# A new order for the opening of an attention and feed-forward kernel: sign vectors with a semaphore of their own, three matmuls on zeros, one fold block moved, weight splits spread out

## Chip, core and metric

The kernel runs on one core of a Trainium2 chip. The metric is the device time of one execution in microseconds, the median of several runs; less is better.

## What is computed

For each of 8 batch rows of 512 tokens x 256 channels:

```python
xn = layernorm(x)                      # no gain, no bias
x  = x + attention(xn) + ffn(xn)
# attention: 32 query heads, 8 key/value heads, head size 64, rotary embedding,
#   causal with a window of 128 keys, softmax, then @ Wo
# ffn: h = fwht(xn * SU_ug) / 64;  up, gate = h @ W_up.T * s1, h @ W_gate.T * s2
#   y = fwht(silu(gate) * up * SU_dp) / 64 @ W_down.T * s3     (fwht: Walsh-Hadamard transform)
```

All tensors are float32.

## The kernel before

Everything on TensorE that carries data from end to end is done with numbers split in two. A value is kept as `hi` (rounded to the matmul's faster float type) and `lo` (the rest), and each product is three matmuls: hi x hi, hi x lo, lo x hi (lines 948 to 950). ScalarE (ACT) makes the hi part, VectorE (DVE) the lo part. Weights are split once, in the first batch row, and query and output weights are written back to memory in split form and loaded from there for later rows.

The Hadamard transforms are folded into the weights. "Fold k" (`fold_gate_up(k)`, line 1024) multiplies the 512 columns of block k of the gate/up weights by the Hadamard matrix: two output tiles of two matmuls each, and each float32 matmul is two passes, so a fold is eight passes in the trace. ACT (`fold_high`, L587) and DVE (`fold_low`, L787) scale these tiles with the input signs `su_in_sb` and split them; tile n may be computed only when `fold_lo` of tile n - 4 is done. The down weights go through three butterfly levels on GpSimd (POOL, L496 and L498), then through four Hadamard products on TensorE (`down_weights`, L1045), are scaled on DVE (`wd_scale`, L824) and split (`wd_high`, `wd_low`).

Each engine runs its own list in program order, and semaphores tie the lists together. The projections and gate/up products alternate over two PSUM banks; the list `USES` sets whose turn it is, and a bank is written again only when the result before has been read.

The opening of the first row, in order:

- SyncE (SP) issues the loads: x, gate/up block 0, key weights, query weights 0, gate/up block 1, down weights, blocks 2 and 3, and so on. Behind them stand `save_wq(0)`, `save_wq(1)` (each waits for the split of these weights), `stack_k(0)`, `load_wq(b, 2)`, `stack_q(0)`, `load_wq(b, 3)`.
- ACT's own queue issues seven small loads: had, ident, scale_gu, su_in, su_mid, cos, sin. The last five count up one semaphore, `consts_in`.
- DVE computes the statistics of x, waits for all five of `consts_in`, scales the two sign vectors, then normalises x (`row_normalised`, L737), then splits.
- ACT takes the square root for the standard deviation, waits for ident, loads the table for silu (L566), makes the hi parts of the key weights (L594), of the first fold tiles, and of the transposed x (`x_high`).
- TensorE does fold 0, the transposes of x, fold 1, key projection 0 (two parts), query projection 0 (two parts), fold 2, fold 3.
- POOL does butterfly level 0, the rotation of key 0 (it waits for DVE's `products` on the key projection), levels 1 and 2, and then the rotation of query 0.

Then the feed-forward part: for j = 0 to 7 TensorE makes gate j and up j (with the query projections 1 and 2 between them at j = 2 and j = 4) and down j - 2; ACT does `silu(j)` and `h_high(j - 1)`; DVE does `hidden(j)` (L841) and `h_low(j - 1)`. In the first row this is mixed with the down weights behind j = 1, and with splits of query weights 2 and 3 behind j = 3 and j = 7. Query weights 1 and the value weights are split ahead of j = 0. Attention over 8 groups follows, and for later rows the same without the weight work.

## Time and profile before

| | |
|---|---|
| median of 3 runs | 1325.61 us (1322.61 to 1327.97) |
| profiled execution | 1322.25 us, span from first to last instruction 1320.5 us |
| busy, share of the span | PE 1257.2 us (95%), DVE 939.3 (71%), ACT 751.9 (57%), POOL 647.9 (49%) |
| mean granted TensorE clock | 0.995 of full speed |
| first 5 us | no TensorE work; from 5 to 10 us, 2.50 of 5 us |

The profile is one execution, recorded on the chip. A timeline row gives the start and length in us, the engine, the line of the kernel, the operation with output and inputs, a count when equal instructions were merged, and in brackets how long the engine had been idle and what released it. "SPq" and "ACTq" are the issuing sides of the DMA queues of these engines. Rows of PE show matmul passes; weight loads have rows of their own (PEld).

### The profile page before, as it was taken

How to read it: one execution, taken by the hardware profiler on the slowest of the kernel's cores; microseconds unless marked ns; L12 is line 12 of the kernel's file. 1: busy time of each engine (PE TensorE's matmuls, PEld its weight loads, DVE VectorE, ACT ScalarE, POOL GpSimd, SP SyncE). 2: the span in 40 equal slices, each digit the busy share in tenths (PEclk: the TensorE clock that was granted, in tenths of full speed). 3: DMA queues.
4: the chain of work that ended last, by engine and by line, in shares of the span. 5: the costliest groups of instructions: out<-in, count | busy, mean ns of one | idle time of the engine just before them, and what ended most of it. 6: DMA issues, size and time to landing. Idle time of an engine off the chain costs nothing.

```text
span 1320.5 us, 38033 instructions
## 1 busy us (share of the span) xinstructions
PE 1257.2 (95%) x14568; PEld 1063.4 (81%) x14568; DVE 939.3 (71%) x1664; ACT 751.9 (57%) x2814; POOL 647.9 (49%) x655
## 2 busy tenths in 40 slices
PE   7899999999999999999999999999999999999997
PEld 3678888788887888878888788888888888887886
DVE  5668984788648886488854888558874688746875
ACT  3357762577626765267643677346763567625775
POOL 4326652366525654266531665326653366523663
PEclk9999999999999999999999999999999999999999
DMA  6315625144142441424322342323423144141431
GB/s 217 88 52 154 189 83 155 57 126 129 50 144 63 116 130 35 142 80 134 95 89 88 95 134 79 104 73 106 130 90 118 47 117 151 53 142 35 128 97 49
DMA packets 72226, 137.56 MB, mean 104 GB/s; under 512 B 15472, under 2 KB 29296, under 8 KB 72048
## 3 DMA queue, kind: packets, MB, share of 16 engines
q1 hardware_dynamic: 70912, 134.41, 33.6%
q8 instruction: 117, 1.92, 0.6%
q10 hardware_dynamic: 1136, 0.73, 0.2%
q14 instruction: 61, 0.50, 0.1%
HBM read 72.17 MB, written 12.58 MB: 64 GB/s over the span
## 4 chain that ended last, share of the span: by engine, by line
PE 84%; DVE 8%; ACT 6%; issue 2%; DMA 1%; ACTq 0%; DVEq 0%
PE PROJ L948 15%; PE PROJ L950 15%; PE PROJ L949 15%; PE S L1099 10%; PE TR L1113 9%; PE O L1130 5%; PE O L1142 4%; PE TR L1130 4%; ACT e_sb L630 3%; PE S L948 2%; PE S L950 2%; PE S L949 2%; ACT pt_sb L640 1%; DVE S L863 1%; DVE v_mix L906 1%
## 5 line engine op out<-in xcount | busy, mean ns | idle before, releaser
L630 ACT ACTIVATE e_sb<-S,negmax 128x128 f32<-128x128 f32 x1024 | 364.8, 382 | 36.7 <-DVE negmax L865 33.9
L507 POOL TENSOR_TENSOR e_sb<-e_sb,rinv 128x512 f32<-128x512 f32 x256 | 264.8, 1042 | 51.7 <-DVE rinv L870 51.2
L515 POOL TENSOR_SCALAR_AFFINE_SELECT p_cur<-pt_sb 128x512 f32<-128x512 f32 x192 | 122.7, 639 | 275.3 <-ACT pt_sb L640 274.1
L640 ACT ACTIVATE pt_sb<-TR 128x512 f32<-128x512 f32 x256 | 154.8, 605 | 168.0 <-PE TR L1113 168.0
L754 DVE TENSOR_TENSOR prod<-PROJ,rope_sb 128x1024 f32<-128x1024 f32 x160 | 193.2, 1211 | 57.0 <-PE PROJ L950 56.9
L630 ACT ACTIVATION_READ_ACCUMULATOR e_sb<-S,negmax 128x1 f32 x1024 | 225.7, 220 | 0.0
L1113 PE MATMUL TR<-ident,e_sb 128*128 128x128 f32 x1024 | 160.6, 280 | 25.3 <-DVE o_lo L710 15.8
L865 DVE TENSOR_REDUCE negmax<-S 128x4 f32<-128x512 f32 x256 | 177.1, 692 | 8.9
L1099 PE MATMUL S<-k_stack,q_stack 64*64 64x64 f32 (+2 forms) x5632 | 179.8, 266 | 1.7 <-ACT e_sb L630 1.7
L483 POOL TENSOR_TENSOR qy<-prod 128x512 f32<-128x512 f32 x64 | 83.9, 1311 | 177.1 <-DVE prod L754 177.0
L948 PE MATMUL PROJ<-wo_ring,o_hi 128*128 128x256 f32 x512 | 155.0, 303 | 16.0 <-DVE xt_lo L710 14.6
L1113 PEld LDWEIGHTS TR<-ident,e_sb 128*128 128x128 f32 x1024 | 116.9, 141 | 63.6 <-issue 32.8
L1099 PEld LDWEIGHTS S<-k_stack,q_stack 64*64 64x64 f32 x5632 | 160.2, 133 | 8.6 <-ACT e_sb L630 5.7
L624 ACT ACTIVATE staging_rest<-PROJ,scale_gu_sb 128x512 f32<-128x512 f32 x64 | 44.2, 690 | 209.3 <-PE PROJ L950 205.4
L949 PE MATMUL PROJ<-wo_ring,o_hi 128*128 128x256 f32 x512 | 144.6, 282 | 0.0
L950 PE MATMUL PROJ<-wo_ring,o_lo 128*128 128x256 f32 x512 | 144.4, 282 | 0.0
L841 DVE SCALAR_TENSOR_TENSOR p_cur<-PROJ,scale_gu_sb,staging_rest 128x512 f32<-128x512 f32 x64 | 48.1, 751 | 130.4 <-PE PROJ L950 130.4
L858 DVE COPY_PREDICATED S<-diagonal_key,S 128x512 f32<-128x512 int8 x192 | 131.5, 685 | 0.0
L948 PE MATMUL PROJ<-xt_hi,wq_ring 128*128 128x512 f32 x256 | 112.7, 440 | 3.9 <-DVE prod L754 3.0
L948 PEld LDWEIGHTS PROJ<-wo_ring,o_hi 128*128 128x128 f32 x512 | 97.7, 191 | 21.2 <-DVE xt_lo L710 18.0
L781 DVE TENSOR_TENSOR acc<-PROJ,acc 128x512 f32<-128x512 f32 x128 | 87.5, 684 | 31.1 <-PE PROJ L950 31.0
L1130 PE MATMUL O<-pt_sb,v_sb 128*64 128x128 f32 x1024 | 106.0, 285 | 1.4 <-ACT pt_sb L640 1.4
(102 smaller groups left out, 2856.5 us busy)
## 6 DMA issues: line engine op xcount, KB each, us to landing
q_stack<-qy SPq DMA_DIRECT2D x512, 64.0 KB, 2.0
wq_ring<-wq_split_d SPq DMA_DIRECT2D x56, 512.0 KB, 4.7
wo_ring<-wo_split_d SPq DMA_DIRECT2D x56, 512.0 KB, 3.5
k_stack<-ky SPq DMA_DIRECT2D x256, 64.0 KB, 2.7
x_in<-x SPq DMA_DIRECT2D x8, 512.0 KB, 4.4
wq_split_d<-wq_ring SPq DMA_DIRECT2D x8, 512.0 KB, 3.9
wo_split_d<-wo_ring SPq DMA_DIRECT2D x8, 512.0 KB, 3.4
out<-acc SPq DMA_DIRECT2D x8, 512.0 KB, 4.9
```

The source lines that it names most:

```text
L507: nc.gpsimd.tensor_tensor(e, e, r, ALU.mult).then_inc(norm_done, 1)
L630: last = nc.scalar.activation(e_sb[:, n % 2, r, :], s_heads(n, 1)[:, r, :], ACT.Exp, bias=negmax[:, n % 2, r:r + 1], accum_out=rowsum[:, n ...
L640: nc.scalar.activation(pt_sb[:, n % 4, :, :], TR[:, :, :], ACT.Copy).then_inc(t_copied, 1)
L754: nc.vector.tensor_tensor(prod[:, 2 * part:2 * part + 2, :], both, rope_sb[:, :, :], ALU.mult).then_inc(prod_done, 1)
L858: nc.vector.copy_predicated(own.rearrange("p r (a k) -> p r a k", a=2), diagonal_key[:, :, :].rearrange("p r (a k) -> p r a k", a=2), diagonal
L865: nc.vector.tensor_reduce(negmax[:, n % 2, :], own, axis=AX.X, op=ALU.max, negate=True).then_inc(max_done, 1)
L948: nc.tensor.matmul(dst, lhs[0], rhs[0], start=first, stop=False)
L949: nc.tensor.matmul(dst, lhs[0], rhs[1], start=False, stop=False)
L950: return nc.tensor.matmul(dst, lhs[1], rhs[0], start=False, stop=last)
L1099: last = nc.tensor.matmul(dst[:, at:at + (blocks - 1) * step + 1:step, :], q_stack[rows, g % 2, slot, i * P + a * HP:i * P + (a + 1) * HP] ...
L1113: last = nc.tensor.transpose(TR[:, r, :], e_sb[:, n % 2, r, :], ident[:, :])
L1130: last = nc.tensor.matmul(O_half[a][odd * D:(odd + 1) * D, s, :, :], v, pt_sb[:, (2 * pair + s) % 4, odd:REP:2, a * HP:(a + 1) * HP], star ...
```

## The change

The sign vectors are loaded right behind the Hadamard matrix, ahead of the identity, and count up a semaphore of their own. DVE normalises x first and then scales the signs. DVE zeroes part of `e_sb` (a tile of the attention, not in use yet) at its very start, and TensorE does three matmuls on it before anything else; their result in PSUM is overwritten later. Fold 2 moves between the key and the query projection, and DVE's and ACT's lists follow. The splits of query weights 1 and of the value weights leave the place ahead of the feed-forward part: query weights 1 now come behind gate/up 1 (ACT: behind silu 0), the value weights at j = 4 (ACT) and j = 6 (DVE). The splits of query weights 2 and 3 come behind j = 2 and j = 6, and the four `wd_low` are spread over j = 2, 2, 3 and 5.

```diff
--- before.py
+++ after.py
@@ -77,7 +77,7 @@
     WO_SLOTS[32] = WO_SLOTS.pop(33)
     WO_SLOTS[33] = (NKV - 1, 0)
 
-    WQ_SPLIT_IN_FFN = {1: 2, 3: 3}
+    WQ_SPLIT_IN_FFN = {2: 2, 6: 3}
     WQ_SPLIT_SLOT = {2: 4, 8: 5, 12: 6, 16: 7}
     WO_SPLIT_SLOT = {2: 0, 3: 1, **{4 * g + 4: g for g in range(2, NKV)}}
 
@@ -228,7 +228,9 @@
 
         ident_in = sem("ident_in")
         had_in = sem("had_in")
+        signs_in = sem("signs_in")
         consts_in = sem("consts_in")
+        warm_in = sem("warm_in")
         wk_in = sem("wk_in")
         wv_in = sem("wv_in")
         wq_raw = [sem("wq_raw0"), sem("wq_raw1")]
@@ -309,7 +311,7 @@
 
         block = ctx.enter_context(nc.Block())
 
-        CONSTS = 5
+        CONSTS = 3
 
         @block.sync
         def _(sp):
@@ -550,10 +552,10 @@
         @block.scalar
         def _(act):
             act.dma_start(had[:, :, :], hadamard.rearrange("s p n -> p s n")).then_inc(had_in, 16)
+            act.dma_start(su_in_sb[:, :], su_in).then_inc(signs_in, 16)
+            act.dma_start(su_mid_sb[:, :], su_mid).then_inc(signs_in, 16)
             act.dma_start(ident[:, :], identity).then_inc(ident_in, 16)
             act.dma_start(scale_gu_sb[:, :], scale_gate_up).then_inc(consts_in, 16)
-            act.dma_start(su_in_sb[:, :], su_in).then_inc(consts_in, 16)
-            act.dma_start(su_mid_sb[:, :], su_mid).then_inc(consts_in, 16)
             act.dma_start(rope_sb[:, 0, :], cos).then_inc(consts_in, 16)
             act.dma_start(rope_sb[:, 1, :], sin).then_inc(consts_in, 16)
             def deviation(row):
@@ -600,9 +602,11 @@
             wq_high(0)
             for n in range(CT, CT * 4):
                 fold_high(n)
-            wq_high(1)
-            act.wait_ge(wv_in, 16)
-            nc.scalar.activation(wv_p[0][:, :, :], kv_stage[:, 1, :, :], ACT.Copy).then_inc(w_hi, 1)
+            act.wait_ge(consts_in, CONSTS * 16)
+
+            def wv_high():
+                act.wait_ge(wv_in, 16)
+                nc.scalar.activation(wv_p[0][:, :, :], kv_stage[:, 1, :, :], ACT.Copy).then_inc(w_hi, 1)
 
             def wd_high(n):
                 act.wait_ge(wd_scaled, n + 1)
@@ -654,18 +658,20 @@
                     nc.scalar.activation(h_p[0][j % 2], h_sb[j % 2], ACT.Copy).then_inc(h_hi_done, 1)
 
                 silu(0)
+                if not b:
+                    wq_high(1)
                 silu(1)
                 h_high(0)
                 if not b:
                     for n in range(FT // 2):
                         wd_high(n)
-                for n in range(1, 4):
-                    hidden = HIDDEN_AFTER[n]
-                    for j in hidden:
-                        silu(j)
-                        h_high(j - 1)
-                    if not b and n in WQ_SPLIT_IN_FFN:
-                        wq_high(WQ_SPLIT_IN_FFN[n])
+                for j in range(2, FT):
+                    silu(j)
+                    h_high(j - 1)
+                    if not b and j == 4:
+                        wv_high()
+                    if not b and j in WQ_SPLIT_IN_FFN:
+                        wq_high(WQ_SPLIT_IN_FFN[j])
                 h_high(FT - 1)
                 if b + 1 < BATCH:
                     deviation(b + 1)
@@ -789,14 +795,15 @@
                     in1=wgu_p[0][:, c, k * 512:(k + 1) * 512].bitcast(fp32), op0=ALU.mult, op1=ALU.subtract
                 ).then_inc(fold_lo, 1)
 
+            nc.vector.memset(e_sb[:, 0, :, :], 0.0).then_inc(warm_in, 1)
             row_stats(0)
-            dve.wait_ge(consts_in, CONSTS * 16)
+            row_rstd(0)
+            for t in range(TT):
+                row_normalised(0, t)
+            dve.wait_ge(signs_in, 2 * 16)
             nc.vector.tensor_scalar(su_in_sb[:, :], su_in_sb[:, :], float(C) ** -0.5, None, ALU.mult).then_inc(su_done, 1)
             nc.vector.tensor_scalar(su_mid_sb[:, :], su_mid_sb[:, :], float(F) ** -0.5, None, ALU.mult).then_inc(su_done, 1)
             dve.wait_ge(su_done, 2)
-            row_rstd(0)
-            for t in range(TT):
-                row_normalised(0, t)
             dve.wait_ge(w_hi, 1)
             low(wk_p[1][:, :, :], kv_stage[:, 0, :, :], wk_p[0][:, :, :]).then_inc(w_lo, 1)
             fold_low(0)
@@ -805,17 +812,20 @@
                 x_low(0, c)
             wq_low(0)
             fold_low(2)
+            fold_low(3)
+            dve.wait_ge(consts_in, CONSTS * 16)
             products(0, "k", 0, 0)
             products(0, "k", 0, 1)
-            fold_low(3)
             fold_low(4)
+            fold_low(5)
             products(0, "q", 0, 0)
             products(0, "q", 0, 1)
-            for n in range(5, CT * 4):
-                fold_low(n)
-            wq_low(1)
-            dve.wait_ge(w_hi, 2)
-            low(wv_p[1][:, :, :], kv_stage[:, 1, :, :], wv_p[0][:, :, :]).then_inc(w_lo, 1)
+            fold_low(6)
+            fold_low(7)
+
+            def wv_low():
+                dve.wait_ge(w_hi, 2)
+                low(wv_p[1][:, :, :], kv_stage[:, 1, :, :], wv_p[0][:, :, :]).then_inc(w_lo, 1)
 
             def wd_scale(n):
                 dve.wait_ge(scale_d_in, 16)
@@ -876,20 +886,24 @@
                     elif b:
                         wo_add(b - 1, NKV - 1, 1)
                 if not b:
+                    wq_low(1)
                     for n in range(FT // 2):
                         wd_scale(n)
-                    for n in range(FT // 2):
-                        wd_low(n)
-                for n in range(1, 4):
-                    if n in (1, 2):
+                for j in range(2, FT):
+                    n = j // 2
+                    if j in (2, 4):
                         products(b, "q", n, 0)
+                        if not b and j == 2:
+                            wd_low(0)
                         products(b, "q", n, 1)
-                    js = HIDDEN_AFTER[n]
-                    hidden(js[0])
-                    for j in js[1:]:
-                        hidden(j)
-                    if not b and n in WQ_SPLIT_IN_FFN:
-                        wq_low(WQ_SPLIT_IN_FFN[n])
+                    hidden(j)
+                    if not b:
+                        if j in (2, 3, 5):
+                            wd_low(j // 2 + j % 2)
+                        if j == 6:
+                            wv_low()
+                        if j in WQ_SPLIT_IN_FFN:
+                            wq_low(WQ_SPLIT_IN_FFN[j])
                 h_low(FT - 1)
                 if b + 1 < BATCH:
                     row_stats(b + 1)
@@ -1025,6 +1039,10 @@
                                                 start=cc == 0, stop=cc == CT - 1)
                     last.then_inc(fold_ready, 1)
 
+            pe.wait_ge(warm_in, 1)
+            for n in range(3):
+                nc.tensor.matmul(S4[:, 3, :], e_sb[:, 0, 0, :], e_sb[:, 0, :, :].rearrange("p r q -> p (r q)"),
+                                 start=True, stop=True)
             pe.wait_ge(had_in, 16)
             fold_gate_up(0)
             pe.wait_ge(ident_in, 16)
@@ -1032,10 +1050,11 @@
                 transposed_x(0, c)
             fold_gate_up(1)
             pe.wait_ge(w_lo, 1)
-            for kind in ("k", "q"):
-                for part in range(2):
-                    project(0, kind, 0, part)
+            for part in range(2):
+                project(0, "k", 0, part)
             fold_gate_up(2)
+            for part in range(2):
+                project(0, "q", 0, part)
             fold_gate_up(3)
 
             def down_weights():
```

## Rows read from the trace of the kernel before

**Rows 1.** Page, part 4: the chain that ended last, share of span by engine.
```profile
PE 84%; DVE 8%; ACT 6%; issue 2%; DMA 1%; ACTq 0%; DVEq 0%
```

**Rows 2.** Waits of TensorE, 0 to 100 us: total, times, longest.
```profile
PE PROJ L948 <- DVE prod L754: 3.0, 2, 2.0
PE TR L1113 <- DVE o_lo L710: 2.5, 1, 2.5
...
PE PROJ L948 <- DVE wq_ring L713: 0.8, 1, 0.8
```

**Rows 3.** Timeline of the opening, 0 to 40: start, length, engine, line.
```profile
3.38 0.48 SPq L357 DMA_DIRECT2D gu_stage<-w_gate_up  x1
...
7.50 5.60 PE L1024 MATMUL S<-gu_stage,had 128*128 128x512 f32 x8 [7.50 <-DMA gu_stage<-w_gate_up]
...
13.58 1.64 PE L979 MATMUL PROJ<-ident,xn 128*128 128x128 f32 x8 [0.49 <-DVE xn L737]
...
15.06 3.60 PE L1024 MATMUL S<-gu_stage,had 128*128 128x512 f32 x8
...
25.48 7.03 PE L1024 MATMUL S<-gu_stage,had 128*128 128x512 f32 x16
```

**Rows 4.** Timeline of the first feed-forward part, 33 to 58.
```profile
33.29 2.40 POOL L498 TENSOR_TENSOR v_sb<-pt_sb 128x1024 f32<-128x1024 f32 x1
...
36.16 2.30 DVE L710 TENSOR_TENSOR wv_lo<-kv_stage,wv_hi 128x1024 fp32r<-128x1024 f32 x1
...
39.17 0.50 PE L948 MATMUL PROJ<-xt_hi,wgu_hi 128*128 128x512 f32 x1 [2.19 <-DVE p_cur L841]
...
39.38 0.51 SPq L327 DMA_DIRECT2D wq_stage<-wq  x1
...
40.68 3.60 PE L1045 MATMUL S<-v_sb,had 128*128 128x512 f32 x8
...
42.21 3.22 DVE L824 SCALAR_TENSOR_TENSOR pt_sb<-S,su_mid_sb,scale_d_b 128x256 f32<-128x256 f32 x8
...
49.03 0.50 PE L948 MATMUL PROJ<-xt_hi,wq_ring 128*128 128x512 f32 x1 [1.96 <-DVE prod L754]
...
57.72 0.69 DVE L713 SCALAR_TENSOR_TENSOR wq_ring<-wq_stage,wq_ring 128x512 fp32r<-128x512 f32 x1
```

**Rows 5.** DMA issues of 0 to 30: KB each, median us to landing.
```profile
ident<-identity ACTq DMA_DIRECT2D x1, 64.0 KB, 5.8
```

**Rows 6.** DMA issues of 2.6 to 3.5 alone, same columns.
```profile
gu_stage<-w_gate_up SPq DMA_DIRECT2D x1, 512.0 KB, 9.0
```

**Rows 7.** DMA issues of 39 to 39.9 alone, same columns.
```profile
wq_stage<-wq SPq DMA_DIRECT2D x1, 256.0 KB, 3.1
```

**Rows 8.** Timeline of ACT's queue, ACT and DVE, 2 to 14.
```profile
2.37 1.29 ACTq L555 DMA_DIRECT2D su_in_sb<-su_in  x1
...
8.15 1.28 ACT L566 ACT_TABLE_LOAD   x1
...
9.56 1.04 ACT L594 ACTIVATE wk_hi<-kv_stage 128x1024 fp32r<-128x1024 f32 x1
...
12.54 0.17 DVE L794 TENSOR_SCALAR su_in_sb<-su_in_sb 128x2 f32<-128x2 f32 x1 [4.64 <-DMA rope_sb<-sin]
...
12.81 1.27 ACT L587 ACTIVATE wgu_hi<-S,su_in_sb 128x512 fp32r<-128x512 f32 x2 [2.22 <-DVE su_mid_sb L795]
```

**Rows 9.** Windows: busy us of PE, PEld, DVE, ACT, POOL; granted clock; DMA share, GB/s.
```profile
100.00:104.00 4.00, 4.00 (x16) 3.27 (x15) 3.60 (x6) 2.29 (x10) 3.34 (x4) 0.57 0.42 107
```

**Rows 10.** Timeline of POOL and DVE, 15 to 21.
```profile
15.45 2.37 POOL L496 TENSOR_TENSOR v_sb<-pt_sb 128x1024 f32<-128x1024 f32 x1 [12.26 <-DMA pt_sb<-w_down]
...
17.98 2.74 DVE L713 SCALAR_TENSOR_TENSOR wq_ring<-wq_stage,wq_ring 128x512 fp32r<-128x512 f32 x1
```

**Rows 11.** Groups by line and shape, 15 to 35: busy us, mean ns.
```profile
L787 DVE SCALAR_TENSOR_TENSOR wgu_lo<-S,su_in_sb,wgu_hi 128x512 fp32r<-128x512 f32 x8 | 5.8, 744 | 4.6 <-ACT wgu_hi L587 4.6
...
L754 DVE TENSOR_TENSOR prod<-PROJ,rope_sb 128x1024 f32<-128x1024 f32 x4 | 4.7, 1211 | 0.0
```

## The prediction

> **What bounds the kernel now.** I read the page first. TensorE (PE) carries 84% of the chain that ended last [rows 1]. So a microsecond comes off the end only if TensorE gets to its steady work earlier, or if a hole in it closes. Next I took the waits of PE in the first 100 us, because the whole change lies in the first image's opening and first feed-forward part. The waits name the holes [rows 2]: 3.0 us for rotary products, 0.8 us for a split of query weights, and 2.5 us for o_lo in the first attention steps. The timeline of that stretch adds two: 2.19 us at 39.17 and 0.49 us at 13.58 [rows 3, 4]. Last I read DMA issues and landings, as the order of the loads is touched too [rows 5, 6, 7].
>
> The opening runs as follows. The first gate/up block lands at 7.5. Fold 0, eight passes, takes 5.60 us, while the eight passes of fold 1 take 3.60 [rows 3]. Transposes start at 13.58, because the normalised rows come late: VectorE (DVE) sat for 4.64 us on one semaphore that counts five small constants, the sine table last, and started its sign scaling at 12.54 [rows 8]. From 15.06 TensorE is nearly full: fold 1, key projection, then 1.04 us (3.0 less 1.96) of waiting for the key products, query projection, and folds 2 and 3 from 25.48 to 32.51 [rows 2, 3, 4]. Then come gate 0, up 0, gate 1 and, after the 2.19 us hole, up 1. The down weights' Hadamard products start at 40.68 and the first part of query projection 1 is read only after DVE has finished its down-weight work, so part 1 starts at 49.03 after 1.96 us [rows 4].
>
> **Part 1, opening, on TensorE.** Three matmuls on zeros give six passes. At twice fold 1's 3.60 / 8 = 0.45 they take at most 6 x 0.90 = 5.4 us; if the memset (one small DVE instruction ahead of work that waits for x anyway) ends by about 1.5, they end by 6.9, before the data at 7.5 [rows 3]. They cost nothing, and at worst a few tenths. Does fold 0 then run at full pace? The granted clock of the first microseconds is printed as the full level, but the passes of fold 0 go at 0.70 us each on average and those of fold 1 at 0.45; in 100 to 104, after 2.53 us without a matmul, the record does show 0.57, a mean of the 1.2 and 2.4 GHz levels [rows 2, 3, 9]. I take the saving as full: 8 x (0.70 - 0.45) = 2.0, with nothing as the other bound. The Trainium skill, "TensorE: Matmul & The Clock Gate", Part 1, says that the array starts throttled and activity releases it; by that rule the 2.0 us are had, and no row here shows zeros doing it.
>
> With it fold 0 ends near 11.1 (13.1 without). The rows are normalised right after their statistics (about 9.8), so the 0.49 wait is gone. Transposes take 1.5 (13.58 to 15.06) and end at 12.6. The next gate/up block was issued at 3.38 and took 9.0, landing at 12.4 [rows 6], just in time. Fold 1 ends at 16.1 instead of 18.66.
>
> ScalarE (ACT) must be ready too. Its table load waits for the identity, which now is issued behind both sign vectors. The issue of su_in alone held the queue for 1.29, a common one takes 0.5; ident took 5.8 to land [rows 3, 5, 8]. It was the second issue of its queue, at about 1.3; near 3.2 gives a landing at 9.0 to 9.4. From there: table load 1.28 and a small activation of 0.2, wk_hi 1.04, two fold_highs 1.27, two x_highs of the same width, and the last x_low some 1.5 behind: 15.9 [rows 8]. That is just under 16.1. The signs stand before the identity in the queue, so they are off the path.
>
> **Part 2, fold 2 between the key and the query projection.** TensorE no longer waits for the key products: fold 2 covers them. Work from 18.66 to 25.48 less the 1.04 wait is 5.8; folds 2 and 3 are 7.03. So gate 0 starts at 16.1 + 5.8 + 7.0 = 28.9 against 32.5: 3.6 earlier. On DVE: the split of the query weights took 2.74 as it had to outlast a POOL instruction (POOL 15.45 to 17.82 and on) [rows 10]. Asked for at 15.9 it runs at the end of that instruction, to 18.4 or 18.5. Behind it stood one fold_low of 0.744 and two products of 1.211; now there are two fold_lows [rows 11]. So the products end at 22.3 (before: 20.72 + 0.74 + 2.42 = 23.9, less small overlaps, 23.7), 1.4 earlier. POOL's key rotation follows them, and the butterfly's rest follows that at POOL's own pace: the last butterfly instruction ended at 33.29 + 2.40 = 35.69, now at 34.3 [rows 4].
>
> **Part 3, wv and the second query split taken out of DVE's way.** Before, that split and wv_lo (36.16 to 38.46) stood ahead of hidden 0, hence the 2.19 hole [rows 4]. After, DVE has only fold_lows before hidden 0. Gate 0 to up 1 is 40.68 - 32.51 less 2.19 and less a short 0.2 for silu = 5.8, so up 1 ends at 34.7, after the butterfly. Down-weight products start at 34.7: 6.0 earlier. That butterfly is the next limit, 0.4 behind.
>
> **Part 4, the second query split now stands after hidden 1, ahead of wd_scale.** hidden 1 to 35.5, h_low to 36.1 or a little over, then the split. Here it may meet the query rotation that POOL starts at 34.3. Rows show the price: a split of 512 elements is 0.69 when POOL rests and up to 2.74 when it must outlast a POOL instruction [rows 4, 10]. I take its end at 38.0 (bounds 36.8 and 38.7). The Trainium skill, "GPSIMD Engine Reference", Specifications, says that GpSimd shares its SBUF interfaces with VectorE instructions that have two SBUF inputs; by it the split would end at the late bound, and the 2.74 row agrees. Eight wd_scales take 3.22 [rows 4], to 41.2, then the product of query part 0, 1.2, to 42.4. Query 1 part 1 starts there: 49.03 - 42.4 = 6.6 earlier. So the DVE wait of 1.96 does not go; it stays near 1.4.
>
> **Part 5, the down-weight lows spread out, query split 2 after hidden 2.** Each wd_low is as long as the split of the same size, 0.69; the first stands between the two products of query 1, while TensorE computes part 1, the other three leave the block for the room behind hidden 2, 3 and 5, and each is ready before the down products that read it (down 2, 4, 6). The split for query 2 stood behind hidden 3 and ended at 58.41, and TensorE waited 0.8 for it [rows 2, 4]. Now it ends before 51, and query 2 starts near 51.0: 7.5 earlier in all. wv and query split 3 go between hidden 6 and 7, where I count on slack: the timeline there holds one hidden and one low per three 1.4 us groups of TensorE, some 2.5 free; even 2.30 for wv_lo [rows 4] is then covered, and if not, costs under 1. On SP the save of wq 1 waits for the later split, and stack_k 0, the load of wq 2 and stack_q 0 stand behind it. The load was issued at 39.38, 3.2 after the split's end (wv_lo followed it at 36.16), and landed 3.1 later [rows 4, 7]; now 38.0 + 6.3 = 44.3. ACT asks for it behind silu 2 and h_high 1 (about 43), and silu 3 behind it is not due before gate 3 at 48. Covered by 4 us.
>
> **Sum.** 3.6 up to gate 0 and 2.4 for the hole before up 1 make 6.0 at the down weights; 0.6 more up to query 1 part 1 (its wait a little shorter): 6.6; and the 0.8 wait at query 2: 7.4, say 7.5. Everything behind this is PE-bound or moves along with it. The profiled execution took 1322.25 (span 1320.5), which gives 1314.8; the median shown is 3.4 above that execution, so 1325.6 - 7.5 = 1318.1. What can be told from no change is 0.5%, 6.6 us; the forecast lies just beyond it.
>
> **Rivals.**
> A. The gain is smaller, 3 to 6 us. Either the identity lands late, or the port is contended more than once. If it lands at 12 instead of 9.3, x_low ends at 18.5; the key products, and with them the butterfly, come 2.2 later, and query 1 part 1 at about 44.8: gain 5.0, time 1320.6. For: its queue-mates now in front are of the smallest pieces, and one of them held the queue for 1.29 [rows 8]. Against: ident's own 5.8 [rows 5]. If the zeros don't raise the pace, fold 0 ends 2.0 later, but the butterfly, h_low and DVE's block at 36 to 42 move far less: query 1 part 1 at 42.9, gain 7.0. So the three matmuls are worth only some 0.5 us here, a point that experiments can settle.
> B. The gain is larger, about 9 to 10. The split meets no POOL instruction (1.2), or the low-clock stretch of 100 to 104 does not come (a mean of 0.57 over 4 us costs 4 x 0.43 = 1.7 us) [rows 9]. Time 1316. For: the timing of both hangs on less than a microsecond. Against: the 2.53 hole ahead of it is DVE's own in-order work, which is untouched.
> C. Slower: the load of query weights 2 lands late, ACT stands on it with silu 3 behind, and every later gate waits. It costs from 48 on; it has eaten the 7.5 at about 56 and decides for slower by 0.5% only beyond 62, 18 us after my estimate. No row shows such a landing (3.1) [rows 7].
> D. Nothing: what is gained up to 51 is given back in the first attention steps. For: DVE is short there, with 2.53 us of hole [rows 2]. Against: that work starts earlier too, and its inputs are no fixed-time loads. Time 1325.
>
> **Chances.** Forecast 0.62, A 0.20, B 0.10, C 0.03, D 0.05. The forecast's own range is 1316.5 to 1320, and a median of a few runs moves by 1 to 2 us, as the three runs from 1322.6 to 1328.0 show. Of the forecast some six in ten fall beyond 0.5%, all of B, a tenth of A: faster 0.53. Same: the rest of the forecast, A and D: 0.43. Slower 0.04. The range of 8 in 10 is 1314.2 to 1322.5: low end B, high end A with a median that is 2 high.
>
> **What would show it.** Right: fold 0's eight passes in 3.5 to 3.7 us, transposes right behind them, near 11; fold 1 from about 12.5; fold 2 before the query matmuls with no wait for products; gate 0 near 29; no 2 us hole before up 1; down weights near 34.7; a wait of 1 to 2 us for products at 42; query 2 near 51 without a wait. Wrong: ACT's table load after 10, a butterfly later than 35, the query split 1 longer than 3 us, a new wait on wq_stage or on wd_lo in 45 to 75, or the attention steps of the first image starting less than 6 us earlier.

## The result: faster by 1.1%, twice what was forecast

The changed kernel took 1310.76 us (median of 4 runs, 1309.9 to 1316.96) against 1326.79 for the kernel before (4 runs, 1322.61 to 1328.13). The ratio is 0.9889, 95% interval 0.9854 to 0.9925. Forecast were 1318.1 and a range down to 1314.2; the time is 3.4 us below that range. The profiled execution took 1316.96 us, with a span of 1315.2 and a mean granted clock of 0.993; of the kernel before it was 1322.25, 1320.5 and 0.995. So the two profiled executions are only 5.3 us apart where the medians are 16.0 apart, and the one of the changed kernel has the lower clock. That is the first clue.

TensorE carries the end as before [rows 1]. The page's chain that ended last:

```profile
PE 85%; DVE 6%; ACT 6%; issue 1%; DMA 1%; SPq 1%; POOL 0%; DVEq 0%; POOLq 0%
```

The opening, from the timeline of the changed kernel (start, length, engine, line, operation):

```profile
1.08 0.48 DVE L798 MEMSET e_sb<- 128x512 f32 x1 [1.08 <-PEq L1255]
...
1.62 5.35 PE L1044 MATMUL S<-e_sb 128*128 128x512 f32 x6 [1.62 <-DVE e_sb L798]
...
3.06 0.93 SPq L359 DMA_DIRECT2D gu_stage<-w_gate_up  x1
...
7.50 3.67 PE L1038 MATMUL S<-gu_stage,had 128*128 128x512 f32 x8 [0.53 <-DMA gu_stage<-w_gate_up]
...
8.32 1.28 ACT L568 ACT_TABLE_LOAD   x1
...
11.01 1.04 PE L993 MATMUL PROJ<-ident,xn 128*128 128x128 f32 x8
...
12.71 3.70 PE L1038 MATMUL S<-gu_stage,had 128*128 128x512 f32 x8 [0.67 <-DMA gu_stage<-w_gate_up]
...
14.53 0.68 DVE L719 SCALAR_TENSOR_TENSOR wq_ring<-wq_stage,wq_ring 128x512 fp32r<-128x512 f32 x1
...
15.69 2.40 POOL L498 TENSOR_TENSOR v_sb<-pt_sb 128x1024 f32<-128x1024 f32 x1 [12.51 <-DMA pt_sb<-w_down]
...
19.05 3.60 PE L1038 MATMUL S<-gu_stage,had 128*128 128x512 f32 x8
...
25.29 3.59 PE L1038 MATMUL S<-gu_stage,had 128*128 128x512 f32 x8
```

The zeros run from 1.62 to 6.97. Fold 0 then takes 3.67 us instead of 5.60, the transposes follow with no wait at 11.01, fold 1 waits 0.67 for its block and starts at 12.71 instead of 15.06 [rows 3]. The split of the query weights 0, 2.74 us before [rows 10], takes 0.68: it starts at 14.53, 1.2 us ahead of the first POOL butterfly. Fold 2 stands between the projections, and folds 2 and 3 end at 25.29 + 3.59 = 28.9, the time forecast for gate 0. Two landings (KB, us from issue):

```profile
ident<-identity ACTq DMA_DIRECT2D x1, 64.0 KB, 6.9
```

```profile
gu_stage<-w_gate_up SPq DMA_DIRECT2D x1, 512.0 KB, 9.6
```

The identity took 6.9 us, not 5.8 [rows 5]; it was issued at 2.37 rather than the assumed 3.2, because the issue of su_in, now second in its queue, took 0.52 (the identity's own, now fourth, 0.86). It landed near 9.3. ACT loaded its table at 8.32, right behind the standard deviation and before that landing, so the table load did not wait for the identity. The block issued at 3.06 landed 9.6 later [rows 6], at 12.7.

The feed-forward part and the first attention steps, timeline again:

```profile
30.16 2.40 POOL L500 TENSOR_TENSOR v_sb<-pt_sb 128x1024 f32<-128x1024 f32 x1
...
34.34 3.60 PE L1064 MATMUL S<-v_sb,had 128*128 128x512 f32 x8
...
35.88 0.69 DVE L719 SCALAR_TENSOR_TENSOR wq_ring<-wq_stage,wq_ring 128x512 fp32r<-128x512 f32 x1
...
40.88 0.50 PE L962 MATMUL PROJ<-xt_hi,wq_ring 128*128 128x512 f32 x1
...
49.44 0.39 PE L962 MATMUL PROJ<-xt_hi,wq_ring 128*128 128x512 f32 x1
...
80.81 0.88 PE L1118 MATMUL S<-k_stack,q_stack 64*64 64x128 f32 x24 [0.17 <-ACT e_sb L634]
...
90.53 0.63 PE L1132 MATMUL TR<-ident,e_sb 128*128 128x128 f32 x4 [2.52 <-DVE o_lo L716]
```

Beside [rows 4] the reader sees: the down-weight products start at 34.34 (40.68 before), query 1 part 1 at 40.88 (49.03), query 2 at 49.44 (58.55 by its wait of 0.81 behind 57.72 + 0.69). The second query split is 0.69 us long: no POOL instruction was in its way, for the butterfly ended at 32.56 and the query rotation at 35.05. The waits of TensorE in 0 to 100 us (total, times, longest) have lost their entries for products, hidden and query split [rows 2]:

```profile
PE TR L1132 <- DVE o_lo L716: 2.5, 1, 2.5
PE S L1044 <- DVE e_sb L798: 1.6, 1, 1.6
PE S L1038 <- DMA gu_stage<-w_gate_up: 1.2, 2, 0.7
```

The scores of the third attention step start at 80.81; in the kernel before they start at 90.01:

```profile
90.01 0.88 PE L1099 MATMUL S<-k_stack,q_stack 64*64 64x128 f32 x24 [0.17 <-ACT e_sb L630]
```

I use this start below as the mark where the changed part ends: 9.2 us of gain. The next hole (a stretch in which TensorE has no matmul running), the wait of 2.52 us for o_lo, is as long as before.

### The profile page after: what moved, and what is told of

Same layout as the page of the kernel before. It is cut to its first block, busy times and chain, and to the rows that moved or that the text cites. A ratio compares the mean times of both kernels' runs of the same rounds, so it can differ in the third digit from the quotient of the medians.

```text
span 1315.2 us, 38048 instructions
## 1 busy us (share of the span) xinstructions
PE 1262.3 (96%) x14574; PEld 1067.0 (81%) x14574; DVE 937.2 (71%) x1665; ACT 752.2 (57%) x2814; POOL 646.1 (49%) x655
## 3 DMA queue, kind: packets, MB, share of 16 engines
q1 hardware_dynamic: 70912, 134.41, 34.3%
q8 instruction: 118, 1.93, 0.7%
## 4 chain that ended last, share of the span: by engine, by line
PE 85%; DVE 6%; ACT 6%; issue 1%; DMA 1%; SPq 1%; POOL 0%; DVEq 0%; POOLq 0%
PE PROJ L962 16%; PE PROJ L964 15%; PE PROJ L963 15%; PE S L1118 10%; PE TR L1132 9%; PE O L1149 5%; PE O L1161 4%; PE TR L1149 4%; ACT e_sb L634 3%; PE S L962 2%; PE S L964 2%; PE S L963 2%; ACT pt_sb L644 1%; DVE S L873 1%; DVE v_mix L920 1%
## 5 line engine op out<-in xcount | busy, mean ns | idle before, releaser
L962 PE MATMUL PROJ<-wo_ring,o_hi 128*128 128x256 f32 x512 | 155.0, 303 | 15.9 <-DVE xt_lo L716 14.6
```

Of the source, the lines that this page charges most:

```text
L962: nc.tensor.matmul(dst, lhs[0], rhs[0], start=first, stop=False)
```

## Experiments

Fifteen runs were made, some of them repeats. Three numbers are read from each. **Mark**: start of the scores of the third attention step of row 0 in the profile. **Time**: median of all executions. **Clock loss** of one execution: its span times one less its mean granted clock; it is the time lost at the lower level, and the clock is printed to three digits, so it is known to 0.7 us. In most profiles up to 1.0 us of it lies in the last 2 to 3 us of the span, where no matmul is left to be slowed (in the kernel before nothing is under way behind 1317.6 but the last store), so it costs nothing there.

| kernel | mark | median time (runs) | mean clock loss | time less loss, mean |
|---|---|---|---|---|
| before, again | 91.29 | 1325.0 (12) | 7.8 | 1316.7 |
| after, again | 80.79 | 1314.5 (6) | 6.8 | 1307.8 |
| after, third sample | 80.48 | 1313.0 (6) | 5.5 | 1307.0 |
| before, o_low first | 91.27 | 1329.0 (11) | 8.8 | 1320.1 |
| after, o_low first | 80.65 | 1319.1 (5) | 9.2 | 1310.2 |
| after without zeros | 81.07 | 1316.0 (4) | 5.9 | 1310.1 |
| after without zeros, again | 81.91 | 1318.1 (7) | 7.7 | 1308.8 |
| after, signs back | 84.61 | 1314.8 (4) | 4.6 | 1311.2 |
| after, fold 2 back | 80.88 | 1315.7 (4) | 8.2 | 1307.1 |
| after, splits back | 86.47 | 1317.8 (5) | 4.0 | 1313.9 |
| before with zeros only | 90.97 | 1327.5 (10) | 11.3 | 1315.1 |
| before with splits only | 84.43 | 1317.5 (7) | 5.5 | 1311.5 |
| before, projection ahead | 91.50 | 1318.6 (12) | 1.7 | 1317.2 |
| after, projection ahead (loss without one execution, see below) | 80.53 | 1309.0 (6) | 0.5 | 1308.2 |
| after, projection ahead, again | 80.30 | 1307.1 (4) | 0.3 | 1307.0 |

### Both kernels again, and a first try at the hole behind o_lo

The kernel before unchanged:

> The kernel before, unchanged, for the granted clock and span of each of its executions. Theory 1 (opening plus clock): the opening of the changed kernel is worth a fixed 9.2 us (attention starts at 80.81 against 90.01), and the rest of the 16 us between the medians is the number of image rows in which the granted clock falls behind the hole at o_lo, 1.7 us each: the executions here should show mean clocks near 0.992 to 0.995 and times that fall with the clock. Theory 2 (something else in the later rows is faster): clocks of the two kernels are alike and the time left at equal clock is 16 us apart.

The changed kernel unchanged:

> The changed kernel, unchanged. Theory 1: time plus or minus the clock loss (span times one less the mean clock) is constant within 1 us, about 1306 to 1308, against 1315 to 1317 for the kernel before; the ratio of medians can come out anywhere between 0.985 and 0.995, by how many of the eight stretches each execution happens to have. Theory 2: ratio 0.988 again with equal clocks.

The two with DVE's order changed in every row:

```diff
                     if u:
                         inverse_sum(2 * u - 1)
-                    if u == 2:
-                        value_mix(3)
                     if u >= 2:
                         o_low(b, u - 2)
+                    if u == 2:
+                        value_mix(3)
```

> The kernel before with one edit in every row's attention: at u = 2 DVE does o_low ahead of value_mix(3), whose two copies were stretched to 1.2 and 1.4 us next to GpSimd. Theory 1: the hole at the transposes behind o_lo (15.8 us over eight rows) nearly closes, and with it the granted clock stays full: 8 x 1.9 = 15 us of holes and 5 to 12 us of clock, so 1300 to 1307, with executions within 1.5 us of each other. Theory 2 (the clock falls for another reason): only the holes' 10 to 15 us, spread between executions as before.

> The changed kernel with the same edit. Theory 1: 1291 to 1298, and 8.5 to 9.5 us under the kernel before with the same edit, since the clock's part is gone from both. Theory 2: the distance between the two stays near 16 us.

The changed kernel again: ratio 0.9914 (0.9894 to 0.9935), executions from 1310.55 to 1319.34. With the clock loss taken off, its executions lie near 1307.8 and those of the kernel before at 1316.5 to 1316.7. So nearly 9 us are fixed, and the rest is clock. Where does the clock go? Windows of the second profile of the kernel before (busy us of PE, PEld, DVE, ACT, POOL, then the granted clock):

```profile
38.00:44.00 6.00, 5.02 (x11) 3.21 (x12) 3.07 (x6) 1.21 (x2) 1.38 (x1) 0.72 0.57 160
...
100.00:106.00 6.00, 4.98 (x20) 4.11 (x20) 5.23 (x9) 3.06 (x13) 4.91 (x6) 0.72 0.51 138
260.00:266.00 6.00, 4.67 (x36) 3.82 (x36) 5.66 (x10) 3.67 (x17) 4.60 (x6) 1.00 0.50 143
```

A mean of 0.72 over 6 us is 6 x 0.28 = 1.7 us lost. The first stretch is behind the hole ahead of up 1:

```profile
38.98 0.62 PE L948 MATMUL PROJ<-xt_hi,wgu_hi 128*128 128x512 f32 x1 [2.19 <-DVE p_cur L841]
```

That hole of 2.19 us stood in the first profile too [rows 4], where the clock did not fall behind it. Among four profiles with this opening and this hole (before, and before again, with o_low first, with the projection ahead) the clock fell there in three, and their marks are 91.3 to 91.5 instead of 90.01: 1.3 to 1.5 us. The other stretches lie behind the o_lo hole of a row, and not behind each: 100 to 106 fell, 260 to 266 did not. In the changed kernel's first profile:

```profile
36.00:42.00 6.00, 5.86 (x22) 3.77 (x21) 5.43 (x11) 3.74 (x6) 0.00 (x0) 1.00 0.50 162
...
88.00:94.00 6.00, 3.48 (x21) 2.96 (x20) 5.64 (x12) 2.46 (x10) 5.85 (x6) 1.00 0.39 109
568.00:574.00 6.00, 5.45 (x22) 4.25 (x24) 4.69 (x8) 4.11 (x18) 4.23 (x5) 0.72 0.43 107
730.00:736.00 6.00, 6.00 (x51) 4.70 (x53) 4.54 (x7) 3.82 (x18) 3.06 (x4) 0.72 0.33 79
```

In 36 to 42 no hole is left and the clock stays full; in 88 to 94 there is a hole with no fall, and in 568 to 574 and 730 to 736 one with a fall. Ahead of the one at 730 stood this:

```profile
729.05 0.63 PE L1132 MATMUL TR<-ident,e_sb 128*128 128x128 f32 x4 [1.89 <-DVE o_lo L716]
```

In the next profile of the same kernel the same places are at full clock, and it is 6.4 us shorter (spans 1315.2 and 1308.8):

```profile
568.00:574.00 6.00, 5.63 (x64) 4.63 (x68) 5.69 (x10) 4.05 (x19) 4.37 (x5) 1.00 0.42 105
730.00:736.00 6.00, 6.00 (x97) 4.94 (x96) 5.42 (x10) 4.17 (x19) 4.45 (x5) 1.00 0.49 142
```

The traces show one thing more about these falls: within an execution they come in runs. In the changed kernel's first profile the waits for o_lo begin at 566.7, 727.2, 887.7, 1048.2 and 1208.7, all five are followed by a fall, and none in the three rows before is. In twelve profiles that have this hole of 1.9 to 2.5 us in each of their eight rows (those of the table without the two edits in attention, and the first pair), 40 of 96 are followed by a fall. From the third row on, 23 of 28 fell where the row before had fallen, and 10 of 44 where it had not. From the second row on, a wait begins some 160.5 us behind the one before it where that one was followed by a fall, and 159.0 where it was not. So once an execution has had one fall it is likely to have several, and a few executions are a poor sample.

The edit on DVE's order fell flat: 4.0 and 4.6 us slower than the unchanged kernels measured beside them. It did shorten the wait for o_lo (0.89 at 88.73 in row 0), but TensorE's next product needs the mixed values that now come later:

```profile
PE O L1149 <- ACT pt_sb L644: 17.6, 9, 2.3
```

The hole had been moved and made longer (2.2 us), and the clock loss was 9 us. So this pair didn't test the theory; it only showed that the two kernels stay 9.9 us apart when both lose about the same clock (8.8 and 9.2).

### The parts of the change, each put back

The three matmuls and the memset left out:

```diff
-            nc.vector.memset(e_sb[:, 0, :, :], 0.0).then_inc(warm_in, 1)
...
-            pe.wait_ge(warm_in, 1)
-            for n in range(3):
-                nc.tensor.matmul(S4[:, 3, :], e_sb[:, 0, 0, :], e_sb[:, 0, :, :].rearrange("p r q -> p (r q)"),
-                                 start=True, stop=True)
```

> The changed kernel without the memset and the three matmuls on zeros. Measure: start of the attention of row 0 (the scores behind 80.8 in the changed kernel; 90.01 before). Theory of the prediction: fold 0 takes 5.6 again and ends 2.0 later, but DVE's block around the down weights hides most of it, so attention starts 0.5 later, 81.3. Rival, from the trace after: the chain is TensorE's own from fold 0 to query 1, with no wait that could take it up, so all 2.1 us arrive: 82.9, and the time without the clock's loss goes from 1307.8 to 1309.9.

The small loads and DVE's list in the old order:

```diff
+            act.dma_start(ident[:, :], identity).then_inc(ident_in, 16)
+            act.dma_start(scale_gu_sb[:, :], scale_gate_up).then_inc(consts_in, 16)
+            act.dma_start(su_in_sb[:, :], su_in).then_inc(consts_in, 16)
+            act.dma_start(su_mid_sb[:, :], su_mid).then_inc(consts_in, 16)
...
             row_stats(0)
+            dve.wait_ge(consts_in, CONSTS * 16)
             (the two sign scalings)
+            row_rstd(0)
+            for t in range(TT):
+                row_normalised(0, t)
```

> The changed kernel with the small loads in the old order and one semaphore, and DVE scaling the signs ahead of the normalisation. Prediction: it cost only the 0.49 us wait when fold 0 was slow, but with a fold 0 of 3.6 us the transposes wait from 11.1 to about 13.6: attention starts 2.5 later, 83.3. Rival: hidden by the wait for gate/up block 1 at 12.7, then 1.5 later at most.

Fold 2 behind the query projection again:

```diff
-            fold_gate_up(2)
             for part in range(2):
                 project(0, "q", 0, part)
+            fold_gate_up(2)
             fold_gate_up(3)
```

> The changed kernel with fold 2 behind the query projection again, and DVE's list to match. Prediction: the wait for the key products comes back with 1.04 us, attention at 81.8. Rival, from the trace after: DVE gets to these products at 17.9 and is through with the first at 19.1, 0.3 after the key projection, since the split of query weights 0 now escapes GpSimd: 0.3 us only, attention at 81.1.

The splits where they were (query 1 and values ahead of the feed-forward part, one block of four wd_low, query 2 and 3 at j = 3 and 7):

```diff
-    WQ_SPLIT_IN_FFN = {2: 2, 6: 3}
+    WQ_SPLIT_IN_FFN = {3: 2, 7: 3}
...
+            wq_low(1)
+            wv_low()
...
+                    for n in range(FT // 2):
+                        wd_low(n)
```

> The changed kernel with all splits where they were: query weights 1 and value weights ahead of the feed-forward part, four down-weight lows in one block, query weights 2 and 3 behind j = 3 and 7. Prediction: the 2.19 us hole before up 1 and the 0.8 us at query 2 come back, less of the rest: 3 to 4 us, attention at 84 to 85. Theory of the clock: holes of 2 us on TensorE in 35 to 50 also let the granted clock fall in some executions, as it did at 38 to 43 in the second profile of the kernel before; so the mean clock loss is larger than in the changed kernel (5.4 us over eleven executions) by about 1 us. Rival: the clock's loss does not depend on the opening.

**Splits**: 5.7 us at the mark (86.47 less 80.8), the largest part by far, and all three old holes are back, longer in sum than [rows 4]:

```profile
35.56 0.50 PE L958 MATMUL PROJ<-xt_hi,wgu_hi 128*128 128x512 f32 x1 [2.66 <-DVE p_cur L852]
...
45.42 0.50 PE L958 MATMUL PROJ<-xt_hi,wq_ring 128*128 128x512 f32 x1 [1.95 <-DVE prod L758]
...
54.97 0.47 PE L958 MATMUL PROJ<-xt_hi,wq_ring 128*128 128x512 f32 x1 [0.80 <-DVE wq_ring L717]
```

The expectation on the clock was missed: with holes of 2.66 and 1.95 us back in the opening, neither was followed by a fall in this profile, and the mean loss is 4.0, not 1 us more than the changed kernel's.

**Signs**: 3.8 us (84.61). The transposes wait, and the clock falls in that place as well:

```profile
7.78 3.67 PE L1038 MATMUL S<-gu_stage,had 128*128 128x512 f32 x8 [0.69 <-DMA gu_stage<-w_gate_up]
13.88 2.21 PE L993 MATMUL PROJ<-ident,xn 128*128 128x128 f32 x8 [2.42 <-DVE xn L743]
```

```profile
12.00:18.00 6.00, 4.12 (x12) 2.71 (x13) 5.10 (x12) 2.98 (x5) 2.22 (x1) 0.72 1.08 365
```

6 x 0.28 = 1.7 of the 3.8 are clock. The rest is the wait: the transposes start 2.87 later than at 11.01, and 0.67 of that would have gone into the wait for block 1 anyway, which leaves 2.2. With the signs back the split of query weights 0 also takes 2.74 us again, behind a POOL instruction that started 0.16 ahead of it:

```profile
18.10 2.36 POOL L500 TENSOR_TENSOR v_sb<-pt_sb 128x1024 f32<-128x1024 f32 x1
18.26 2.74 DVE L719 SCALAR_TENSOR_TENSOR wq_ring<-wq_stage,wq_ring 128x512 fp32r<-128x512 f32 x1
```

**Fold 2**: 0.1 us (80.88), or 0.3 if one allows for fold 1, which started 0.25 earlier in that execution (12.46) because its block had landed; the time less loss, 1307.1, is no different. The wait for the key products was 1.04 us before [rows 2]; with the split of query weights 0 out of POOL's way 0.42 of it is left (at 18.96) with fold 2 back in its old place.

**Zeros**: 0.3 us, and 0.5 more since in that execution the first block landed at 7.00 instead of 7.50. By time less loss it is 2.3, so it is taken up again below.

### Parts alone, and the hole filled

The kernel before with one part each:

> The kernel before with the memset and the three matmuls on zeros alone. Fold 0 ends at 11.2, but the rows are normalised no earlier, so transposes start at 13.6 as before: attention starts at 90.0, nothing gained, and with a hole of 2.4 us before the transposes the clock may fall there. Rival: the fold's 2.0 us arrive, 88.0.

> The kernel before with only the splits moved (query weights 1 and value weights, the four down-weight lows, query weights 2 and 3). Putting them back cost the changed kernel 5.7 us at the start of attention; if the parts add up, this alone brings attention from 90.0 to 84.3 and the time without the clock's loss from 1316.5 to about 1311. By the prediction's own terms (2.4 for the hole before up 1, 0.8 at query 2, 0.6 at query 1) it would be 3.8, attention at 86.2.

Zeros alone gain nothing (ratio 1.0018, 0.9997 to 1.0039). Fold 0 is fast, the rows are no earlier, and the gain turns into a hole with a fall of the clock behind it (13 to 19 us: 0.72):

```profile
7.59 3.67 PE L1026 MATMUL S<-gu_stage,had 128*128 128x512 f32 x8 [1.64 <-DMA gu_stage<-w_gate_up]
13.74 2.00 PE L981 MATMUL PROJ<-ident,xn 128*128 128x128 f32 x8 [2.49 <-DVE xn L738]
```

The splits alone bring 84.43, where 84.3 was expected from putting them back: 5.6 to 5.7 from either side, not the 3.8 that the prediction's terms make.

Then the hole behind o_lo, with work that TensorE has to do anyway: at u = 2 part 0 of a query projection goes ahead of the transposes that wait.

```diff
+                        if u == 2:
+                            fill(2 * u)
                         if u:
                             transposes(2 * u - 2)
-                        fill(2 * u)
+                        if u != 2:
+                            fill(2 * u)
```

> The changed kernel, and in every row's attention at u = 2 TensorE computes part 0 of query projection 4 (some 1.4 us) ahead of the transposes that wait for o_lo, instead of behind them. Theory (the clock is lost behind this hole): the eight holes of 1.9 to 2.5 us shrink to about 0.5 to 1.1, so up to 11 us come off, and the granted clock stops falling at them: mean clock 0.998 or more, executions within 2 us of each other, median 1296 to 1300. Rival: the fall has nothing to do with the hole; then 1300 to 1304 with the same spread of 3 us and clocks of 0.990 to 1.0.

> The kernel before with the same edit. If the clock behind the holes is what stood between the 9.2 us of the opening and the 16 us first measured, this pair differs by 9.2 us plus what the falls at 38 to 43 us cost the kernel before (up to 1.3): 9 to 10.5, both with a small spread. If the opening of the changed kernel has another effect on the later rows, the pair differs by 12 or more again.

The ratio to the kernel before is 0.9891 (0.9863 to 0.9919) for the changed kernel with it and 0.9957 (0.9942 to 0.9971) for the kernel before with it; the pair is 1318.6 - 1309.0 = 9.6 us apart. Half of my theory held. The clock stays full in the rows:

```profile
568.00:574.00 6.00, 4.68 (x63) 3.57 (x66) 5.69 (x10) 4.09 (x19) 4.47 (x5) 1.00 0.43 108
728.00:734.00 6.00, 5.12 (x91) 4.30 (x92) 5.54 (x11) 4.56 (x20) 4.14 (x5) 1.00 0.37 87
```

But the holes' own 11 us did not come off. The waits of TensorE in 200 to 1300 us, changed kernel first:

```profile
PE TR L1132 <- DVE o_lo L716: 13.2, 7, 1.9
...
PE TR L1132 <- ACT pt_sb L644: 7.8, 10, 0.8
PE O L1149 <- ACT pt_sb L644: 1.4, 2, 1.2
```

```profile
PE TR L1132 <- ACT pt_sb L644: 14.0, 18, 0.8
...
PE O L1149 <- ACT pt_sb L644: 2.9, 9, 1.2
PE TR L1132 <- DVE o_lo L716: 2.3, 7, 0.3
```

The 13.2 us of waiting for o_lo became 2.3, and the waits for ACT's copies grew from 7.8 + 1.4 to 14.0 + 2.9, so 7.7 of the 10.9 us came back in other waits, in pieces of at most 0.8 us (one of 1.2). That other engines set the pace of these steps is my reading of it; where the other 3.2 went I didn't find. The time less loss did not fall: 1317.2 against 1316.7 in the kernel before, 1308.2 (and 1307.0 in a second sample, below) against 1307.0 to 1307.8 in the changed one. What the edit gains is clock alone: 6.6 us of time in the kernel before, 6.2 of them in the recorded loss. (One of the ten executions of this version of the changed kernel, 1314.0 us with a recorded clock of 0.948, stands apart; I have no explanation for it.)

### A larger sample

> The changed kernel once more, for a larger sample. The start of attention is 9.2 us earlier (10.5 where the kernel before has its fall at 38 to 43), and the first measurement gave 16 us. If the rest of the first difference was the draw of a small sample, the pooled median difference comes down to 9 to 12; if the changed kernel loses less clock behind its holes by nature, its mean loss stays 3 us or more under that of the kernel before, and the difference stays at 12 to 14.

> The version with part 0 of query projection 4 ahead of the transposes again, on the same chip as the changed kernel: it should be faster than it by the changed kernel's mean clock loss, 3 to 6 us, at 1308 to 1310, with no run's time above 1311 except by another cause.

> The changed kernel without the three matmuls on zeros again. Its trace gave the start of attention only 0.3 us later (with the first block landing 0.5 earlier), its time without the clock's loss 2.3 us more in four executions. Theory: the wait for gate/up block 1 absorbs most of the slow fold 0, so 0.5 to 0.8 us and the 2.3 was the draw; rival: the zeros are worth 2 us, by a later landing in most executions.

The changed kernel: ratio 0.9908 (0.989 to 0.9925). Pooled over its three samples, 17 executions have a median of 1312.8 and a mean clock loss of 5.4. The executions of the kernel before in these jobs, 81, have 1325.2 and 8.2. So the difference is 12.4 us by this: 8.7 of it at full clock (medians; 9.1 by means), about 3 of clock. The first 16.0 was partly the draw: its medians, 1326.79 and 1310.76, lie 1.6 above and 2.0 below the pooled ones, and the changed kernel's first sample had a loss of only 3.7. The filled version has 0.9869 (0.9855 to 0.9884), 1307.1, 5.9 under the changed kernel beside it, and is the fastest of all: 18 us under the kernel before.

The zeros: in this profile the block landed at 7.21, fold 0 took 5.76, and the mark is 81.91, 1.4 us behind the 80.48 of the changed kernel beside it.

```profile
7.21 5.76 PE L1037 MATMUL S<-gu_stage,had 128*128 128x512 f32 x8 [7.21 <-DMA gu_stage<-w_gate_up]
...
13.68 3.60 PE L1037 MATMUL S<-gu_stage,had 128*128 128x512 f32 x8
```

Fold 1 starts 1.35 later than in that kernel (12.33); of fold 0's 2.1 us the wait for the second block took the rest. The two profiles say 0.3 and 1.4, the times less loss 1.3 to 2.3. I put the zeros at 1 to 2 us; how much in one execution depends on the two landings.

## Why the prediction was wrong

**Direction and mechanism: right.** TensorE's path in the opening and the first feed-forward part carried to the end. In eight profiles (before, before again, after, after again, without zeros, signs back, fold 2 back, splits back) span less mark less clock loss behind the mark (summed over the windows of the profile) is 1223.8 to 1225.9, whatever the opening did. The two of the kernel before lie lowest (1223.8 and 1224.5), so of the 9.2 us at the mark about 1 may be given back behind it; that agrees with the 8.7 to 9.1 at full clock.

**Opening, part 1: right.** 2.0 for the fold was 1.93 (5.60 less 3.67), the 0.49 wait went, fold 1's end was 16.4 for 16.1. That it would be paid little was foreseen, in rival A, with a wrong reason: I put the cover at DVE's block around 36 to 42, and it was the wait for the second block. **Part 2: right in sum, wrong in its cause.** Gate 0 came at 28.9 as forecast, but fold 2's place is worth 0.1 to 0.3. Zeros and sign order were rightly summed together, for neither pays alone: without the signs the fast fold 0 only makes a wait of 2.4 us (0.49 beside the slow fold), with a fall of the clock behind it in both profiles that have it.

**Parts 3 to 5, the term that was mis-sized.** I let both splits meet POOL (2.5 and 1.9 us) and had query 1 part 1 at 42.4; both missed it, and it came at 40.88. For the first split the fault lies chiefly in part 1: ACT's table load, which I let wait for the identity, did not, so DVE came to the split at 14.53 instead of 15.9, ahead of POOL's instruction at 15.69. The key products ended at 20.48 for 22.3 and the butterfly at 32.56 for 34.3, and POOL was through with the query rotation at 35.05, before the second split began at 35.88. That the second split doesn't need the first for this is shown by the kernel before with the splits only: there the first met POOL (2.80 us) and the second still took 0.68. The bound 1.2 below was named in part 4 and stood as rival B; the split ended at 36.57, just under it. Query 2 was forecast at 51.0 and came at 49.44. So the path gained 9.2 by the marks, not 7.5. The GpSimd rule weighed in part 4 (the Trainium skill, "GPSIMD Engine Reference", Specifications) isn't contradicted: 0.69 against 2.74 is what missing or meeting one costs here. In these traces meeting it cost DVE this much where POOL was first. In the changed kernel without the zeros the split started at 14.98 and POOL's instruction at 15.12: the split took 0.68 all the same, and POOL's took 2.78 instead of 2.4.

**The step that failed** is "everything behind this is PE-bound or moves along with it", taken as if the time behind the opening were a constant. Its work is; its clock isn't. The kernel before loses 8.2 us on average, the changed one 5.4, and single executions lose 0 to 13. I saw one such stretch (0.57 in 100 to 104 [rows 9]) and priced it as the whole of the effect, 1.7 us in rival B, instead of asking how many holes of its kind there are in eight rows and in the opening itself. Of the 8.5 us between 16.0 and the forecast 7.5, some 3.6 are the draw of two small samples, 1.2 to 1.7 the mis-sized splits, and the remaining 3 to 4 mostly the clock; without the draw the changed kernel's 1312.8 still lies under the stated range.

The change closes two holes of 2 us in the opening, of which one was followed by a fall in three of four profiles: 1.3 to 1.5 us when it happens. That would account for about 1 of the 3 us. It is not shown: with such holes put back the mean loss was 4.0, no more than without them. Why the changed kernel also lost less in its rows is open. Chance alone is an unlikely reason: its three samples lost 3.7, 6.8 and 5.5 on average, the five of the kernel before 7.8 to 8.8, and the difference of 2.8 is three times its standard error (0.9). But the versions with other openings lost anything from 4.0 to 11.3, in no order that follows their gain. Falls come in runs, so when the first one comes weighs more than how many holes there are; what brings the first one I could not find in any row.

Two sums of the prediction don't come out as printed: six in ten of the forecast, B and a tenth of A make 0.49 for faster, not 0.53, and the rest of the forecast, A and D make 0.48 for the same, not 0.43. The forecast time doesn't rest on them.

## What to carry to other kernels

In this kernel a hole of about 2 us on TensorE could cost twice: itself, and some 1.7 us at the lower clock behind it. Count such holes over the whole kernel before a gain is sized, and compare executions by time less clock loss. Work that must be done anyway and is ready can be put into a hole even where other engines set the pace; here it gained no work time but kept the clock. And a part's worth depends on what stands next to it: the zeros are worth nothing without the sign order, the fold's place 0.3 us at most once the split before it is quick.

## What the runs showed of the hardware that was not expected

- The same kernel's executions differ by up to 10.6 us (1308.73 to 1319.34), mostly through the granted clock: their loss runs from 0 to 13 us, their time less loss from 1306.1 to 1309.9.
- A fall to the 1.2 GHz level came behind holes of 1.9 to 2.5 us, and not behind each of them (40 of 96 in the rows; not behind one of 2.66); behind a row with a fall the next mostly had one too (23 of 28, against 10 of 44); where the o_lo hole was cut into pieces of at most 0.8 us, none came in the rows of three profiles, though waits of up to 1.6 us for xt_lo stayed.
- Matmuls on zeros raise the clock as others do: six passes took 5.35 us, and the next eight 3.67, against 5.60 with none in front [rows 3]. The Trainium skill, "TensorE: Matmul & The Clock Gate", Part 1, has it that activity releases the throttle; the runs agree.
- The record prints the full clock (1.00) in the first 12 us of every profile, while the first three or four of fold 0's passes without the zeros start 0.85 to 1.0 us apart, and most behind the zeros 0.43; this loss is not in the clock column.
- Of two instructions of DVE and POOL that met, the one that started first kept its time: 0.68 for the split and 2.78 for POOL where the split was 0.14 ahead, 2.74 and 2.36 where POOL was 0.16 ahead.
